# Delta heads of a decoder layer: the lower triangle built next to the key product, decays one slot further ahead, inverse norms by a GpSimd power, the substitution first in its slot

## The reference

```python
q = _causal_conv(x @ Wq.T, cw_q, cb_q)          # four taps, then silu; k and v likewise
g = exp(-exp(A_log) * softplus(x @ Wa.T + dt_bias)); beta = sigmoid(x @ Wb.T)
q = _l2norm(q); k = _l2norm(k)                   # x / max(sqrt(sum x*x), 1e-12), per head
def step(S, (q_t, k_t, v_t, g_t, beta_t)):
    error = v_t - g_t * (S^T k_t)
    S = g_t * S + k_t (beta_t * error)^T
    return S, S^T q_t
o = o * rsqrt(mean(o*o) + eps) * norm_w * silu(x @ Wg.T);  return o @ Wo.T
```

## Time and profile before

| what | value |
|---|---|
| median of three executions | 4026.02 us |
| profiled execution, its own time | 4027.95 us |
| its span | 4026.1 us |
| TensorE / VectorE / ScalarE / GpSimd busy, whole span | 86% / 54% / 44% / 37% |
| stretch 130 to 1990 us: TensorE busy | 1730.86 of 1860.00 us |
| same stretch: VectorE, ScalarE, GpSimd busy | 1152.23, 1041.58, 1145.39 us |
| same stretch: mean granted TensorE clock | 0.97 |

### The profile page before, as it was taken

How to read it: one execution, slowest core, us unless ns; L and a number is a source line. 1 busy time by engine, 2 the same in 40 slices (tenths; PEclk the granted TensorE clock), 3 DMA queues, 4 the chain that set the end, 5 groups by cost and what they waited for, 6 DMA issues and landing times. The chain is left out here.

```text
span 4026.1 us, 62497 instructions
## 1 busy us (share of the span) xinstructions
PE 3447.7 (86%) x19682; PEld 2733.0 (68%) x19682; DVE 2154.6 (54%) x4501; ACT 1774.1 (44%) x4509; POOL 1503.7 (37%) x2924
## 2 busy tenths in 40 slices
PE   3799999999999999999799488869979999974993
PEld 1688888888888888888677244458856666654441
DVE  2566666666666666666432577745536546532223
ACT  2456555555655555556421155534434434431110
POOL 2466665656666666666300100045532000003203
PEclk9899999999999999999899699989989999985996
DMA  2111111111111111111243400023344120115324
GB/s 65 36 48 38 34 41 44 40 44 41 44 41 33 41 39 45 44 41 28 85 120 119 165 11 13 13 66 108 120 158 154 53 83 31 52 63 203 126 91 154
DMA packets 399009, 279.41 MB, mean 69 GB/s; under 512 B 137520, under 2 KB 323760, under 8 KB 397776
## 3 DMA queue, kind: packets, MB, share of 16 engines
q1 hardware_dynamic: 391504, 257.42, 21.2%
q0 software_dynamic: 5120, 16.78, 1.3%
q10 hardware_dynamic: 2304, 4.20, 0.3%
HBM read 179.22 MB, written 99.09 MB: 69 GB/s over the span
## 5 line engine op out<-in xcount | busy, mean ns | idle before, releaser
L506 PE MATMUL gd_PJ<-xn_lead,gd_w_rest 128*128 128x512 f32 x1024 | 449.6, 439 | 17.6 <-DVE gd_w_rest L669 17.6
L506 PE MATMUL gd_PJ<-xn_lead,gd_w_lead 128*128 128x512 f32 x1024 | 411.7, 402 | 0.0
L506 PE MATMUL gd_PJ<-xn_rest,gd_w_lead 128*128 128x512 f32 x1024 | 409.2, 400 | 0.0
L676 DVE SCALAR_TENSOR_TENSOR gd_conv<-gd_pre,gd_cur_a,gd_conv 128x512 f32<-128x512 f32 x384 | 298.1, 776 | 154.6 <-ACT gd_conv L821 147.5
L940 POOL TENSOR_TENSOR gd_T<-gd_T,gd_prod 32x14 f32<-32x14 f32 (+6 forms) x896 | 328.4, 366 | 70.2
L937 POOL TENSOR_TENSOR gd_prod<-gd_L,gd_T 32x14 f32<-32x14 f32 (+6 forms) x896 | 316.5, 353 | 70.2
L516 PE MATMUL gd_B<-gd_W,gd_Lo 128*128 128x64 f32 x1536 | 210.2, 283 | 95.5 <-DMA gd_W<-turned_image 95.5
L820 ACT COPY gd_pre<-gd_PJ 128x512 f32<-128x512 f32 x192 | 111.3, 580 | 380.3 <-PE gd_PJ L506 379.5
L516 PEld LDWEIGHTS gd_B<-gd_W,gd_Lo 128*128 128x128 f32 x1536 | 199.8, 203 | 103.3 <-DMA gd_W<-turned_image 89.7
L506 PEld LDWEIGHTS gd_PJ<-xn_lead,gd_w_rest 128*128 128x128 f32 x1024 | 199.0, 194 | 47.6 <-DVE gd_w_rest L669 21.8
L506 PEld LDWEIGHTS gd_PJ<-xn_lead,gd_w_lead 128*128 128x128 f32 x1024 | 197.3, 193 | 45.9
(11 more groups left out here) (400 smaller groups left out, 8842.3 us busy)
## 6 DMA issues: line engine op xcount, KB each, us to landing
turned_queries_keys<-f_wq SPq DMA_DIRECT2D x16, 1280.0 KB, 6.0
gd_T<-inverse_image SPq DMA_DIRECT2D x64, 256.0 KB, 2.9
gd_W<-turned_image SPq DMA_DIRECT2D x64, 256.0 KB, 3.3
gated_outputs<-gd_og SPq DMA_DIRECT2D x64, 256.0 KB, 2.6
go_ogt<-gated_outputs SPq DMA_DIRECT2D x16, 1024.0 KB, 6.8
sa_qT<-turned_queries_keys SPq DMA_DIRECT2D x16, 1024.0 KB, 5.6
gathered<-sa_blank SPq DMA_DIRECT2D x39, 256.0 KB, 7.2
ms_xr<-gathered SPq DMA_DIRECT2D x39, 256.0 KB, 2.7
```

The costliest lines, as they stand in the source:

```text
L506: mm = pe.matmul(bank, w_parts[wp][:, j, k, :], rhs, start=(k == 0 and wp == 1), stop=(k == KT - 1 and wp + xp == 0))
L676: nc.vector.scalar_tensor_tensor(out=conv[:, j], in0=pre[:, parm, j, :, d:d + P], scalar=cur[:, 4 * j + d:4 * j + d + 1], in1=conv[:, j], ...
```

## The change

- The key product of chunk n+2 (`each(Bk[4], k_c, k_c)`) moves in TensorE's slot from behind `u_sum` to ahead of the V projection.
- VectorE's work on it (diagonal, sum, maximum, once, twice, Lo) moves from several places at the slot's end to one place, ahead of the three taps of V.
- Sqrt on ScalarE and reciprocal on VectorE go. VectorE clamps the squared norm at 1e-24, and GpSimd raises it to the power -1/2, once per slot for keys (`k_rnorm`) and once for queries (`q_rnorm`).
- The decay argument and its Exp run for chunk n+3 instead of n+2, so a flag has3 and a first slot `slot(-1, 1, ...)` that does this alone come in; GpSimd reads the decay rows directly from the table of all heads.
- GpSimd begins its slot with the substitution (`start_solve`, `solve`); Sd, the key power and the decay rows come behind it.
- The turning of a weight in chunks 1 and 2 moves ahead of the decay argument on TensorE, and its copy ahead of Exp on ScalarE.

```diff
--- before.py
+++ after.py
-slot(-1, 2, False, False, True, True)
-slot(-1, 3, False, True, True, True)
+slot(-1, 1, False, False, False, True, True)
+slot(-1, 2, False, False, True, True, True)
+slot(-1, 3, False, True, True, True, True)
 with eng.Fori(0, LAST) as i:
     for c in range(CH):
-        slot(i, c, True, True, True, True)
+        slot(i, c, True, True, True, True, True)
 for c in range(CH):
...
             each(Bk[1], q_c, tiles(S), oi_sum)
+    if has2:
+        pe.wait_ge(k_silu, n + 3)
+        if has1:
+            pe.wait_ge(lo_ready, n + 2)
+        each(Bk[4], k_c, k_c, kk_done)
     if has1:
...
-    if has2:
-        pe.wait_ge(k_silu, n + 3)
-        if has1:
-            pe.wait_ge(lo_ready, n + 2)
-        each(Bk[4], k_c, k_c, kk_done)
...
-    if has2:
-        pe.wait_ge(lgm_ready, n + 3)
-        if has1:
-            pe.wait_ge(d_exp, n + 2)
+    if back and more and c in (1, 2):
+        pe.wait_ge(v_pre, n + 4)
+        turn_weights(i + 1, JK if c == 1 else JV)
+    if has3:
+        pe.wait_ge(lgm_ready, n + 4)
+        if has2:
+            pe.wait_ge(d_exp, n + 3)
...
-    if back and more and c in (1, 2):
-        pe.wait_ge(v_pre, n + 4)
-        turn_weights(i + 1, JK if c == 1 else JV)
     if back:
         pe.wait_ge(o_ready, n + 2)
-        if has2:
-            pe.wait_ge(d_exp, n + 3)
+        if has3:
+            pe.wait_ge(d_exp, n + 4)
...
         tap(n + 1, parm, PQ, cur_a, (2,), q_tap)
+    if has2:
+        dve.wait_ge(kk_done, n + 3)
+        nc.vector.tensor_tensor(diag[:], Bk[4][:, :, :], ident.unsqueeze(1).to_broadcast([P, B, P]), ALU.mult).then_inc(kdiag, 1)
+        dve.wait_ge(kdiag, n + 3)
+        nc.vector.tensor_reduce(root[:, 0, :], diag[:], AX.X, ALU.add).then_inc(k_len, 1)
+        dve.wait_ge(k_len, n + 3)
+        nc.vector.tensor_scalar(root[:, 0], root[:, 0], 1e-24, None, ALU.max).then_inc(k_max, 1)
+        dve.wait_ge(k_rnorm, n + 3)
+        both = cur_k[:, P_BETA:P_G].rearrange("p (j n) -> p j n", j=2)[:, :, c2 * B:c2 * B + B]
+        by = rn[:, parm, 0, :].unsqueeze(1).to_broadcast([P, 2, B])
+        if back:
+            dve.wait_ge(vb_ready, n + 1)
+        nc.vector.tensor_tensor(once[:, par], both, by, ALU.mult).then_inc(once_ready, 1)
+        dve.wait_ge(once_ready, n + 3)
+        nc.vector.tensor_tensor(twice[:, par], once[:, par], by, ALU.mult).then_inc(scales_done, 1)
+        dve.wait_ge(scales_done, n + 3)
+        dve.wait_ge(d_exp, n + 3)
+        for b in range(B):
+            st = nc.vector.scalar_tensor_tensor(out=Lo[:, par, b, :], in0=Bk[4][:, b, :], scalar=twice[:, par, 0, b:b + 1],
+                                                in1=D[:, b, :], op0=ALU.mult, op1=ALU.mult)
+        st.then_inc(lo_ready, 1)
+    if has1:
         dve.wait_ge(v_halo, n + 2)
...
-    if has2:
-        dve.wait_ge(kk_done, n + 3)
-        nc.vector.tensor_tensor(diag[:], Bk[4][:, :, :], ident.unsqueeze(1).to_broadcast([P, B, P]), ALU.mult).then_inc(kdiag, 1)
-        dve.wait_ge(kdiag, n + 3)
-        nc.vector.tensor_reduce(root[:, 0, :], diag[:], AX.X, ALU.add).then_inc(k_len, 1)
         dve.wait_ge(o_sum, n + 1)
+        dve.wait_ge(q_rnorm, n + 1)
...
-    some = slice(0 if has2 else 1, 2 if has1 else 1)
-    if has1 or has2:
-        dve.wait_ge(root_done, n + 3)
-        nc.vector.tensor_scalar(root[:, some], root[:, some], 1e-12, None, ALU.max).then_inc(max_done, 1)
-        dve.wait_ge(max_done, n + 3)
-        nc.vector.reciprocal(rn[:, parm, some], root[:, some]).then_inc(rnorm_done, 1)
...
+    if has1:
+        dve.wait_ge(q_len, n + 2)
+        nc.vector.tensor_scalar(root[:, 1], root[:, 1], 1e-24, None, ALU.max).then_inc(q_max, 1)
...
-        act.wait_ge(rnorm_done, n + 2)
+        if back:
+            act.wait_ge(q_rnorm, n + 1)
...
         silu(PV, vT[:, :], v_silu)
-    if has2:
-        act.wait_ge(darg, n + 3)
-        if has1:
-            act.wait_ge(d_cut, n + 2)
-            act.wait_ge(lo_ready, n + 2)
+    if back and more and c in (1, 2):
+        lead_weights(i + 1, JK if c == 1 else JV)
+    if has3:
+        act.wait_ge(darg, n + 4)
+        if has2:
+            act.wait_ge(d_cut, n + 3)
+            act.wait_ge(lo_ready, n + 3)
         nc.scalar.activation(D[:], Bk[0][:, :, :], ACT.Exp).then_inc(d_exp, 1)
-    some = slice(0 if has2 else 1, 2 if has1 else 1)
-    if has1 or has2:
-        if has2:
-            act.wait_ge(k_len, n + 3)
-        if has1:
-            act.wait_ge(q_len, n + 2)
-        nc.scalar.activation(root[:, some], root[:, some], ACT.Sqrt).then_inc(root_done, 1)
...
-    if back and more and c in (1, 2):
-        lead_weights(i + 1, JK if c == 1 else JV)
...
+def start_solve(m, later_one):
     pool.wait_ge(l16_in, m * 16 + 16)
     if later_one:
         pool.wait_ge(t16_out, m * 32)
     nc.gpsimd.tensor_tensor(T16[:], L16[:], below[:], ALU.mult).then_inc(solving, 1)
+
+def solve(m):
+    at = m * (2 * STEPS)
...
+    h3, c3 = (i if c < 1 else i + 1), (c + 3) % CH
+    if has2 and c == 2 and back:
+        pool.wait_ge(k_tap, (n + 2) * 3)
+        pool.wait_ge(once_ready, n + 2)
+    if has1 and c == CH - 1 and back:
+        pool.wait_ge(kd_ready, n + 1)
+        pool.wait_ge(extra_done, n + 1)
+    if has1:
+        start_solve(n + 1, back)
+    if has2 and c == 2:
+        row(cur_k, h2, head_k)
+    if has1 and c == CH - 1:
+        row(cur_a, h1, head_a)
+    if has1:
+        solve(n + 1)
     if back and c > 0:
-        if c == 2 and has2:
-            pool.wait_ge(k_tap, (n + 2) * 3)
-            pool.wait_ge(once_ready, n + 2)
-        if c == CH - 1 and has1:
-            pool.wait_ge(kd_ready, n + 1)
         pool.wait_ge(extra_done, n + 1)
         pool.wait_ge(s_ready, n + 1)
         nc.gpsimd.tensor_tensor(Sd[:], S[:], bc(end[:, par, :], P), ALU.mult).then_inc(sd_ready, 1)
-    if has1 and c == CH - 1:
-        row(cur_a, h1, head_a)
     if has2:
-        if c == 2:
-            row(cur_k, h2, head_k)
-        if has1:
-            pool.wait_ge(darg, n + 2)
+        pool.wait_ge(darg, n + 3)
+        pool.wait_ge(k_max, n + 3)
+        nc.gpsimd.tensor_tensor(rn[:, parm, 0], root[:, 0], minus_half[:], ALU.pow).then_inc(k_rnorm, 1)
+    if has3:
         for part, col in zip(lgm, (P_LG, P_LGR)):
-            tt = nc.gpsimd.tensor_tensor(part[:], bc(cur_k[:, col + c2 * B:col + c2 * B + B], P),
-                                         later.unsqueeze(1).to_broadcast([P, B, P]), ALU.mult)
+            at = col + c3 * B
+            lg = ptab[:, bass.ds(h3, 1), at:at + B].rearrange("p o n -> p (o n)")
+            tt = nc.gpsimd.tensor_tensor(part[:], bc(lg, P), later.unsqueeze(1).to_broadcast([P, B, P]), ALU.mult)
         tt.then_inc(lgm_ready, 1)
-    if has1:
-        solve(n + 1, back)
...
-        pool.wait_ge(rnorm_done, n + 3)
+        pool.wait_ge(q_max, n + 2)
+        nc.gpsimd.tensor_tensor(rn[:, parm, 1], root[:, 1], minus_half[:], ALU.pow).then_inc(q_rnorm, 1)
+        pool.wait_ge(q_rnorm, n + 2)
...
+nc.gpsimd.memset(minus_half[:], -0.5).then_inc(cleared, 1)
```

34 lines of the change are left out of this document (9 added, 25 removed).

## The result

The changed kernel takes 4144.6 us (median of four, 4137.2 to 4161.0) against 4029.8 us beside it: ratio 1.029, interval 1.025 to 1.034. It is slower, where 3937 us was forecast. The profiled execution has a span of 4149.5 us.

A forecast was written before the change was run, and what follows sets the result against it. TensorE was taken as the bound, waiting late for the inverse. From 4027.95 us: minus 83 (DMA waits), 39 (clock), 12 (weights), plus 41 (U) and 3 (power) gave 3938, stated as 3937 us; 8-in-10 range 3900 to 4050 us.

The forecast's parts named there:

- the loop's sum: Substitution, key power, scales, Lo, taps, ScalarE, next substitution: 26.4 us + p, hidden under TensorE's 27.6 us slot up to p = 1.2.
- p: Time of one GpSimd power, for keys or queries: taken as 0.5 us, between 0.20 and 4.0 us.
- rival 2: Loop longer than counted, by the power or slower substitutions: 3999 us at one us over the bound, chance 0.14.
- the signs of being wrong: Power's mean over 1.2 us, TensorE waiting for decay rows every slot, or VectorE waiting behind a running substitution in most slots.
- The head period: Time of one head, four slots, in the changed profile: expected near 111 us, from 116.2 us before.
- the DMA waits: TensorE's 32 waits for the DMA bringing the inverse back (gd_W): all 83.0 us to go, by earlier Lo and substitution first.
- The clock's 39 us: TensorE's slow clock after the DMA waits: 2.5 us in fifteen slots and 1.7 us in the last head, gained if waits go.
- The wait for U: TensorE loses the key product as cover while ScalarE copies U: 0.66 us in 62 slots, 41 us lost.
- the weights: Weights turned earlier in chunks 1 and 2: 12 us of the 17.6 us of waits for a weight's second part to go.
- Rivals 1 and 5: 1: GpSimd's power is long, up to 4111 us, chance 0.18; 5: code switches on GpSimd, 4024 us or more, 0.03.
- the forecast's picture: Changed profile: gd_W waits gone or under 10 us, a U wait some 60 times, no slow matmuls, head period near 111 us.

The follow-up runs named there:

- the third experiment: The changed kernel with the query-key product moved up between the turned queries and the output sum, to cover U's copy: 4223.0 us, 78 us slower than the changed kernel.

## Why the prediction was wrong

The step that failed is the loop's sum, "26.4 + p" against a slot of TensorE of 27.6 us: "So up to p = 1.2 us the loop is hidden". The loop exists, but its terms for the scales, the power and the taps were too small, and the slot of TensorE that should hide it was not independent of it: the same power, scales and taps hold back Exp and Pm, and with them TensorE. By the loop's terms, in the turn shown:

- osq to the first instruction 0.2 (forecast 0.3, with 0.2 for the row copy), substitution 13.8 (14.6), Sd 1.0 (0.8): right or a little high.
- GpSimd then waits 2.2 us for the maximum of the key norms; the sum had nothing for that. It is not a link of this loop but the mark of the other one, by way of TensorE, for which the forecast had no sum. Over all slots it is 54.2 us, 0.9 for each of 62.
- p is 1.01 us against 0.5: inside its bounds and under 1.2, so the test "wrong if the power's mean is over 1.2" did not fire. The run without the power is 57 us faster.
- Scales and Lo took 3.2 us, from 951.81 to 954.98, against 1.6. This is the mis-sized term: their durations came from the earlier trace rows, where GpSimd ran no long product beside them. Over all slots the means of `once` and `twice` are 1.61 + 0.77 = 2.4 us, against 0.4 us before: 2.0 us a slot. Holding GpSimd's products back gave 59 us.
- V's taps 2.7 (2.3), ScalarE 6.7 (6.6).
- The 3.3 us of issue at the loop's top, once a head, had no term; the trace of the kernel before has only 3.4 us of it in all.

The turn is 30.85 us instead of 26.9, 28.6 of it without the wait for the maximum; the average slot is 31.1 us. That is rival 2 ("the loop is longer than I count"), priced there at one us over the slot where it was three. None of the signs of being wrong came in full: TensorE waited for the decay rows in 26 slots, not in every one, and VectorE's wait for the power (114.8 us) is 4.1 us in chunk 0's slot, behind a running substitution, but 1.2 us in the other three, hardly more than the power. The head period was the sign that told.

The other steps. That the DMA waits go was right (0 of 83.0 us left), but the substitution alone, moved first, makes the kernel 163 us slower. "I take all 83.0 us" priced the wait that goes and not what the moved step now stands in front of: the decay rows, and V's taps. The clock's 39 us did not come: 7.3 us a head at the lower level stand against 6.8 before, since waits such as the 2.35 us for Pm bring the lower level back. They came where the loop was open. The wait for U was right (39.1 for 41), the weights were not: w_rest went from 17.6 to 35.1 us in place of 12 less, and the part alone is 19 us slower. Rivals 1 and 5 fell: 1.01 us each, for keys and queries alike, and no switch can be seen, while the gap of 3 us at the loop's top belongs to the jump, since the kernel before shows it with memsets alone.

With the loop open and the decay products last, the forecast's picture came out: 111.2 us a head, no waits for gd_W, 35.1 us for U, 6.1 us for w_rest where 5.6 were left in the sum, the granted clock at 1.00. So the terms outside the loop were about right. That 3948.5 us lies so near to 3937 is in part luck: that kernel still had GpSimd's wait for both scales, and without it (and with the halos in one instruction) the time is 3910.1 us, 27 under the forecast.

## What to carry to other kernels

Putting an engine's longest chain first in its slot closes a loop with whatever it waited for last: add that loop link by link, each with its neighbour on the other engine, and ask whether the links also hold back the engine that is meant to hide it. Here the loop was 0.7 us under the slot by the sum and 3 us over in fact; putting off its smallest instruction opened it. A duration read where the other engine is idle is a lower bound. Waits that merge into one longer wait can cost more than their sum, by the clock (78 us in the third experiment). Moving a long product away from one small victim can put it beside another, so look at all of the neighbour's rows.

## What the runs showed of the hardware

- GpSimd's power of 128x4 takes 1.01 us, against 0.20 us for a product of the same shape.
- A VectorE product of 128x8 with two SBUF inputs takes 0.17 us alone, 1.0 us beside a 128x512 product on GpSimd, and up to 3.75 us beside a series of them. The Trainium skill (SBUF — State Buffer, SBUF: two separate sides) calls the shared ports an exclusive lock, held by the first for its whole instruction. The row agrees with that and adds that the loser may lose several times in a row.
- VectorE's three taps of 128x512 take 2.33 us in the kernel before and in the fastest one, 2.83 us beside Dm, and 5.78 us beside Sd, the decay products and the halos (substitution first alone).
- A loop body of 309 or more listed rows on GpSimd brings 70 instruction packets more, and gaps at 14 jumps (46.8 us in all and up to 3.6 in the changed kernel, 59.3 and up to 4.9 with the products held back, 35.7 with the memsets); one of 302 rows has 3.4 us in all. With the memsets, where GpSimd has time, they cost nothing that can be measured.
- The granted clock of TensorE stayed 1.00 through a wait of 0.78 us and fell after waits of 2.20 and 2.35 us, but it also stayed 1.00 with waits of 2.00 and 2.94 us (changed kernel, 895 to 929 us).
